# Moving twenty-eight places in the step table of a two-layer AdaLN kernel

## What is computed

```python
h = _layernorm(x) * (1 + ca) + sa
x = x + ga * _L0_attn_ref(h, ...)   # 16 heads of width 8, 4 key/value groups, relative-position bias, softmax
h = _layernorm(x) * (1 + cb) + sb
x = x + gb * _L0_ffn_ref(h, ...)    # routing: 4 of 16 experts; each silu(x W1 + b1) * (x W3 + b3), then W2
h = _layernorm(x) * (1 + ca) + sa   # layer 1
x = x + ga * _L1_attn_ref(h, ...)   # state-space layer: causal conv of 4, softplus step, scan over time, 256 x 16 states
h = _layernorm(x) * (1 + cb) + sb
x = x + gb * _L1_ffn_ref(h, ...)    # three matrices in a row (folded into one here), tanh
```

## Time and profile before

| | us |
|---|---|
| median of three runs | 2800.82 |
| profiled execution | 2800.82 |
| its span, first to last instruction | 2798.9 |
| PE busy | 2359.9 (84%) |
| DVE busy | 1940.0 (69%) |
| POOL busy | 1736.1 (62%) |
| ACT busy | 1631.4 (58%) |

### The profile page before, as it was taken

One profiled execution on the slowest core, in us unless ns is written; L12 is line 12 of the kernel. 1 busy time (PEld: TensorE's weight loads), 2 busy tenths in 40 slices (PEclk: granted clock), 3 DMA queues, 4 the chain that ended last, 5 costly groups with the idle time before them and its releaser, 6 DMA issues. The chain is left out here.

```text
span 2798.9 us, 37099 instructions
## 1 busy us (share of the span) xinstructions
PE 2359.9 (84%) x9792; PEld 1213.6 (43%) x9792; DVE 1940.0 (69%) x3181; ACT 1631.4 (58%) x4156; POOL 1736.1 (62%) x2247
## 2 busy tenths in 40 slices
PE   5889998989898999989889898989899998958433
PEld 3555544444444444444444444444444444422100
DVE  3444567686777768686776768686786868666776
ACT  3655566666666666666666666666666665533332
POOL 1012257585867858585866758586785857587543
PEclk9999999999999999999999999999999999978665
DMA  7424374665546565565546456555656465333442
GB/s 137 48 43 77 58 141 96 122 121 128 117 98 126 110 138 103 118 122 128 112 91 133 99 121 123 121 117 108 123 102 144 104 121 114 107 91 91 113 122 68
DMA packets 497981, 304.96 MB, mean 109 GB/s; under 512 B 349818, under 2 KB 416298, under 8 KB 497322
## 3 DMA queue, kind: packets, MB, share of 16 engines
q1 hardware_dynamic: 497772, 302.59, 52.9%
HBM read 242.21 MB, written 26.74 MB: 96 GB/s over the span
## 5 line engine op out<-in xcount | busy, mean ns | idle before, releaser
L1128 POOL TENSOR_TENSOR work<-work,bc 128x512 f32<-128x512 f32 x512 | 650.3, 1278 | 104.9 <-PE bank L1164 82.4
L1134 DVE TENSOR_TENSOR_SCAN work<-bank,work 128x512 f32<-128x512 f32 x512 | 621.2, 1213 | 109.3 <-POOL work L1128 83.5
L873 POOL TENSOR_TENSOR zh<-zh,w_bc 128x512 f32<-128x512 f32 x256 | 326.8, 1277 | 581.9 <-DVE zh L866 579.5
L1141 POOL TENSOR_TENSOR work<-work,bc 128x512 f32<-128x512 f32 x448 | 581.2, 1303 | 74.9 <-DVE work L1134 74.9
L1117 ACT ACTIVATE bank<-work,neg_a 128x510 f32<-128x510 f32 x512 | 351.5, 687 | 460.8 <-DVE work L1134 448.5
L532 PE MATMUL bank<-ke,q_all 96*128 96x256 f32 x2048 | 555.2, 395 | 12.0 <-DMA q_all<-q_rows 12.0
L549 ACT ACTIVATE probs<-bank,nmax 128x256 f32<-128x256 f32 x1024 | 473.6, 470 | 134.0 <-DVE nmax L539 131.9
L539 DVE TENSOR_REDUCE nmax<-bank 128x2 f32<-128x512 f32 x512 | 348.7, 681 | 233.0 <-PE bank L532 221.9
L532 PEld LDWEIGHTS bank<-ke,q_all 96*128 96x128 f32 x2048 | 382.1, 197 | 214.1 <-issue 163.2
L860 PE MATMUL bank<-h_b,w_t 128*128 128x512 f32 x512 | 297.4, 664 | 118.0 <-DVE zh L851 102.2
L559 PEld LDWEIGHTS bank<-ident,probs 128*128 128x128 f32 x2048 | 255.5, 144 | 242.6 <-issue 168.1
(11 more groups left out here) (192 smaller groups left out, 2528.4 us busy)
## 6 DMA issues: line engine op xcount, KB each, us to landing
work<-dt_rows SPq DMA_DIRECT2D x256, 512.0 KB, 5.3
w_bc<-w_rows_d SPq DMA_DIRECT2D x256, 256.0 KB, 4.4
ke<-ke SPq DMA_DIRECT2D x128, 256.0 KB, 5.0
bc<-bc_rows SPq DMA_DIRECT2D x64, 256.0 KB, 6.6
x_in<-in_x SPq DMA_DIRECT2D x32, 256.0 KB, 5.0
q_all<-q_rows SPq DMA_DIRECT2D x512, 8.0 KB
dt_rows<-step SPq DMA_DIRECT2D x16, 512.0 KB, 3.7
dt_rows<-step SPq DMA_DIRECT2D x32, 256.0 KB, 2.4
```

The lines of the kernel that those rows point to most:

```text
L873: nc.gpsimd.tensor_tensor(zh[:, n % 3, :], zh[:, n % 3, :], w_bc[:, n % WB, :], ALU.mult).then_inc(m_p, 1)
L1128: nc.gpsimd.tensor_tensor(hb[at % HB], ring[n % RING][:, 1, :], bc[:, s, :], ALU.mult).then_inc(s_dbx, 1)
L1134: nc.vector.tensor_tensor_scan(hb[at % HB], decay_bank(p, m)[:, :], hb[at % HB], 0.0, ALU.mult, ALU.add).then_inc(s_h, 1)
L1141: nc.gpsimd.tensor_tensor(hb[at % HB], hb[at % HB], bc[:, SG + batch(m)[2], :], ALU.mult).then_inc(s_hc, 1)
```

## The change

Only numbers of the table change (and the first and last step of the loop). 28 pieces get another step, most by one or two. In the order of the engines: on SP `x_a`, `x_res`, `a_store`, `m_fetch` and `f_store`; on PE `a_inverse`, `a_query`, `a_back`, `b_turned`, `m_weights`, `s_rows` and `f_turned`; on ACT `s_decay` (all 512 decays one step later), `a_keys`, `a_values_in`, `b_turned`, `m_weights`, `m_end` and `s_norm`; on DVE `s_end`, `m_up` (all 256 one step earlier), `a_end`, `s_silu` and `s_step`; on POOL `a_root`.

```diff
-            a_out_tensor=[79, 144], a_out_scalar=[79, 145], s_end_vector=[447, 499],
+            a_out_tensor=[79, 144], a_out_scalar=[79, 145], s_end_vector=[448, 500],
...
-            a_query_tensor=-34, f_end_tensor=531, a_back_tensor=148, b_turned_tensor=157, m_logits_tensor=164,
...
+            a_query_tensor=-33, f_end_tensor=531, a_back_tensor=150, b_turned_tensor=159, m_logits_tensor=164,
...
-            f_mix_tensor=527, s_decay_scalar=-1, m_tanh_scalar=2, a_turn_scalar=8, a_exp_scalar=3, a_values_scalar=42,
...
+            f_mix_tensor=527, s_decay_scalar=0, m_tanh_scalar=2, a_turn_scalar=8, a_exp_scalar=3, a_values_scalar=42,
...
-            a_max_vector=1, m_up_vector=4, m_silu_vector=2, a_inverse_vector=34, a_scale_vector=42, a_stats_vector=-88,
...
+            a_max_vector=1, m_up_vector=3, m_silu_vector=2, a_inverse_vector=34, a_scale_vector=42, a_stats_vector=-88,
```

More of the change, by code:

```diff
@@ L266, in build @@
         GROUP_STEPS = 4 * CPG
-        FIRST, LAST = -101, STEPS * (PAIRS - 1) + 535
+        FIRST, LAST = -102, STEPS * (PAIRS - 1) + 538
         AT = dict(
-            a_out_tensor=[79, 144], a_out_scalar=[79, 145], s_end_vector=[447, 499],
-            a_spread_sync=[[-28, -28, -12, 4], [20, 36, 52, 68]], a_scatter_sync=[[-22, 4], [37, 69]], x_a_sync=-99,
-            x_res_sync=107, a_store_sync=-34, m_store_sync=178, m_fetch_sync=-13, s_rows_sync=377,
-            s_rows_in_sync=[378, 380, 384, 386], s_store_sync=[372, 374], s_fetch_sync=-14, f_store_sync=531,
+            a_out_tensor=[79, 144], a_out_scalar=[79, 145], s_end_vector=[448, 500],
+            a_spread_sync=[[-28, -28, -12, 4], [20, 36, 52, 68]], a_scatter_sync=[[-22, 4], [37, 69]], x_a_sync=-100,
+            x_res_sync=104, a_store_sync=-35, m_store_sync=178, m_fetch_sync=-11, s_rows_sync=377,
+            s_rows_in_sync=[378, 380, 384, 386], s_store_sync=[372, 374], s_fetch_sync=-14, f_store_sync=534,
@@ L280, in build @@
[L280 to L283 removed]
+            a_inverse_tensor=42, s_sum_tensor=6, a_turned_tensor=-48, a_keys_tensor=-42, a_values_in_tensor=-37,
@@ new lines, in build @@
+            a_query_tensor=-33, f_end_tensor=531, a_back_tensor=150, b_turned_tensor=159, m_logits_tensor=164,
+            m_weights_tensor=178, m_back_tensor=326, s_turned_tensor=340, s_in_x_tensor=[348, 356], s_step_tensor=[364, 365],
+            s_rows_tensor=374, s_in_z_tensor=[390, 397], f_out_tensor=508, f_back_tensor=513, f_turned_tensor=524,
+            f_mix_tensor=527, s_decay_scalar=0, m_tanh_scalar=2, a_turn_scalar=8, a_exp_scalar=3, a_values_scalar=42,
+            a_norm_scalar=-51, a_turned_scalar=-42, a_keys_scalar=-40, a_values_in_scalar=-35, a_query_scalar=-33,
@@ L291, in build @@
-            f_root_gpsimd=517, s_step_vector=[366, 370],
+            s_silu_vector=[352, 360], s_zgate_vector=[392, 401], f_res_vector=514, f_stats_vector=518, f_end_vector=533,
+            s_read_gpsimd=4, m_weigh_gpsimd=5, s_input_gpsimd=-3, a_root_gpsimd=-83, b_root_gpsimd=155, s_root_gpsimd=330,
+            f_root_gpsimd=517, s_step_vector=[364, 368],
         )
```

9 lines of the change are left out of this document (3 added, 6 removed).

## The result

The changed kernel takes 2827.82 us (median of seven runs, 2815.03 to 2832.09), the kernel before 2800.41 us in the seven runs beside them (2788.27 to 2810.37). The ratio is 1.0102, with a 95% interval of 1.0074 to 1.013. The change made the kernel slower by 1%. The forecast of 2795 us is wrong, and wrong in its direction.

What follows compares the result with a forecast made beforehand. PE was taken as nearly full (146.90 of 160 us), with the chain to `b_turned` and DVE's routing barring shorter pairs. Sum: 2800.8 + 3 (regular pairs) + 5 (clock) - 14 (lock) = 2795 us; range 2764 to 2828.

Steps and rivals of the forecast that it cites:

- the clock's: Behind PE's wait ahead of `b_turned`: clock may halve, losing 1.7 us, in one pair in four: +5 us, bounds 0 and +20.
- The rival of 2828: Clock falls ahead of the routing in every second pair, and the up ahead of MAX meets slow PE: +27, chance 0.14.
- The wait itself: PE's wait ahead of `b_turned`: gains of 0.46 (`a_back`) and 0.7 us (earlier up) lengthen it from 1.12 to about 1.9.
- `h_b` ahead of the tanh, +0.6: On ACT: the copy delays the tanh, the silu and the routing stretch, +0.6 us a pair, bounds 0.3 and 0.8.
- the up ahead of MAX, +0.3: On DVE: the up, moved ahead of three small pieces, may meet PE still at work: 0 to +0.7 us, taken as +0.3.
- the tanh ahead of its decay, -0.6: End of the routing: the silu no longer waits 0.61 us for the tanh, -0.6 us a pair, bounds -0.6 and 0.
- The up ahead of the scan, +0.4: On DVE: it now waits for PE's up, where it waited 0.77 us for POOL: +0.4 us a pair.
- The slack that should have taken up two thirds of the loss: DVE's 2.0 us of idle time in the next stretch absorbs two thirds of +0.7 us, leaving +0.2 a pair.
- The lock, -14: DVE and POOL's shared lock: L1173 leaves the offset that stalls it, saving 3 x 4.8, about -14 us; bounds -14 and +55.
- `f_turned`, 0, and the step sizes, 0: PE's 0.48 us ahead of `f_turned` turns up again behind a decay; step sizes' later DVE work is covered by idle time.
- Over 160: a new wait repeats in each pair: Sign that the forecast is wrong: pairs over 160 us apart, where 157.3 plus or minus 1 was expected.
- The rival of closing waits: Four waits of PE close: -52 us, 2749, if all go, about 2766 with half and the stalls gone; chance 0.28.

Runs made afterwards that it cites:

- e1_fill: The changed kernel with twelve identity transposes on TensorE ahead of `b_turned`, where it would wait: 2788.28 us, 0.994 to the kernel before.
- e8_nodecay: The changed kernel with `s_decay_scalar` back at its old number, -1, and nothing else: 2819.27 us, 1.0061 to the kernel before.
- e3_back148: The changed kernel with `a_back_tensor` back at its old place, 148: 2822.08 us, 1.0072 to the kernel before.
- e7_back150: The kernel before with `a_back` alone moved behind the transposes (`a_end` and `b_turned` renumbered, which moves nothing): 2809.56 us, 1.0012.
- e5_decay0: The kernel before with the decay's number alone changed, so ACT puts an expert's tanh ahead of the decays: 2843.51 us, 1.0147.
- e6_hb: The kernel before with `h_b` copied ahead of the tanh of the 13th expert (`b_turned_scalar` 159): 2805.43 us, 1.0033.
- e2_up4: The changed kernel with DVE's up back at its old number (`m_up_vector` 4): 2828.74 us, 1.0064 to the kernel before.
- e4_up3: The kernel before with the number of DVE's up alone changed (`m_up_vector` 3): 2795.1 us, 0.998.
- e12_fill2: The changed kernel with twelve identity transposes ahead of `b_turned` and eight ahead of the routing weights: 2787.46 us, 0.9959 to the kernel before.
- e10_fill4: The changed kernel with four identity transposes ahead of `b_turned`: 2799.11 us, 0.9995 to the kernel before.
- e13_nodecayw: The changed kernel with `s_decay_scalar` back at -1 and eight identity transposes ahead of the routing weights: 2799.03 us, 0.9994 to the kernel before.
- e9_bfill: The kernel before with twelve identity transposes on TensorE ahead of `b_turned`: 2796.99 us, 0.9987.

## Why the prediction was wrong

**The step that failed is the clock's.** "One pair in four: 12/4 x 1.7 = +5 us." The mechanism, the place and the wait of 1.9 us were named; the sum then took a quarter of the pairs. Eleven of twelve fell. Measured by e1_fill: the twelve pairs take 1901.3 us with the filler and 1931.4 without, so the clock costs +30 us in them, 2.5 a pair. The other mistake in the term is its price. 1.7 us is the work lost in one slow stretch, and that is what one of 3.4 us costs (1.6); but seven of the eleven are twice as long (6.8 us) and cost 3.2. In eight of the eleven the 14th expert's up is slow besides, all or in part, which costs up to 0.9 more. The argument against the rival, that PE may be slowed in the scores alone, is refuted by the gate's 2.08 us.

The trace of before held what was needed. All pairs are copies of each other, so a wait that comes once comes in every pair. The fall does not come in every one: in the kernel before, the wait of about 2.23 us ahead of the 14th expert's up stands in all twelve pairs and the clock falls behind it in eight. That rate was there to be counted, and a quarter had no basis. The trace also had a price for a fall that is not hidden: its pair of 160.3 us (875.2 to 1035.5) has no stall. There the clock held behind the 2.23 us and fell at the up behind the weights, as in e8_nodecay. PE and the window, kernel before:

```profile
902.47 1.12 PE L860 MATMUL bank<-h_b,w_t 128*128 128x512 f32 x2 [2.23 <-DVE zh L851]
...
913.01 2.07 PE L860 MATMUL bank<-h_b,w_t 128*128 128x512 f32 x2 [1.29 <-DVE zh L851]
```
```profile
912.30:919.00 6.70, 5.99 (x14) 3.94 (x14) 4.46 (x5) 4.17 (x13) 6.70 (x7) 0.50 0.54 141
```

That is 3.0 us for one fall (0.66 of it may be L1173, at 1.81 us in this pair), not 1.7 in one pair of four. The rival of 2828 (0.14) had the right cause and nearly the measured time, partly by luck. Its falls in every second pair were too few. Its 0.7 for an up ahead of MAX that meets a slow PE is real (0.9, e1_fill), but does not come in every pair, and it does not say what its second 0.7 stands for.

**The wait itself** was forecast at about 1.9 and came at 1.97. Its working was half wrong: `a_back`'s 0.46 us has no part in it (e3_back148: 1.94, e7_back150: 1.10). The move of the tanh makes all of it (e5_decay0: 1.93, e8_nodecay: 1.09), by bringing the tanh 1.6 us and the up 0.8 us forward against a chain that starts when it starts. The gain of `a_back` stands ahead of the 12th expert's up instead.

**`h_b` ahead of the tanh, +0.6; the up ahead of MAX, +0.3; the tanh ahead of its decay, -0.6.** Together they were +0.3. e6_hb shows 0 for the first alone: its 0.6 took a later tanh for a later routing, and the pair did not lengthen. The other two show in the start of the up behind the weights, in pairs in which the 14th expert's up is fast. Before, it starts 37.81 us behind the pair's end. In e2_up4, which has the tanh ahead of its decay but not the up ahead of MAX, it starts at 37.07, so that term is -0.7. In e1_fill, which has both, it starts at 37.61, so the up ahead of MAX costs 0.5. Where the 14th expert's up is slow, the two starts are 37.47 and 38.55, and it costs 1.1. The prediction had 0 and 0.7 for these two cases: the difference between them was right, the level was 0.5 too low.

**The up ahead of the scan, +0.4.** Right: the next up starts 44.8 us behind the pair's end in e1_fill, 44.4 before. It (L862 in e1_fill) waits 1.10 us where L860 waited 0.61. The one after it waits 1.53 where it was 0.95. From e1_fill's timeline, against the second group, which is the timeline of the kernel before:

```profile
1547.23 1.13 PE L862 MATMUL bank<-h_b,w_t 128*128 128x512 f32 x2 [1.10 <-DVE zh L853]
1555.86 0.70 PE L862 MATMUL bank<-h_b,w_t 128*128 128x512 f32 x1 [1.53 <-DVE zh L853]
```
```profile
1877.97 1.12 PE L860 MATMUL bank<-h_b,w_t 128*128 128x512 f32 x2 [0.61 <-DVE zh L851]
1886.03 1.12 PE L860 MATMUL bank<-h_b,w_t 128*128 128x512 f32 x2 [0.95 <-DVE zh L851]
```

The slack that should have taken up two thirds of the loss did not: a pair is 0.8 to 0.9 us longer, and the prediction had 0.2. In twelve pairs e1_fill lies 13.7 us above 12 x 157.3 (1901.3 - 1887.6), where the prediction had +3. Some 5.5 of them are falls further back, one at the up behind the weights (1.7) and five at the 14th expert's (0.3 to 1.0); the rest, some 8, is the order, and by e2_up4 it is the up's number.

**The lock, -14.** Right in size: the two stalls in the twelve pairs had cost 11.4 us, the third lay in the filling, and L1173 has no 4.8 left (e4_up3, e2_up4: the up's number does it). The sum took 4.8 us for a stall where the text beside it read 5.5 from the pairs. In a stall L1173 takes 3.7 us longer (4.82 against 1.15), and the pair 5.5 to 6.0. The rest goes with the clock, which falls behind each stall. Window of the kernel before, behind the stall at 1399.07:

```profile
1403.60:1410.50 6.90, 4.25 (x10) 2.75 (x11) 6.64 (x9) 3.01 (x9) 3.81 (x4) 0.51 0.00 1
```

What the sum lacked is that leaving the bad offset is not the same as leaving POOL. L1173 starts at the very moment at which POOL begins an operation, and takes 1.81 us. DVE, then POOL, in the changed kernel:

```profile
1576.04 1.81 DVE L1173 SCALAR_TENSOR_TENSOR z_gate<-x_slots,d_par,z_gate 128x512 f32<-128x512 f32 x1
```
```profile
1574.80 1.27 POOL L1128 TENSOR_TENSOR work<-work,bc 128x512 f32<-128x512 f32 x1
1576.04 2.94 POOL L1141 TENSOR_TENSOR work<-work,bc 128x512 f32<-128x512 f32 x2
```

1.81 is one operation of POOL (1.26) and 0.55 us behind its end; before, L1173 took 1.15 in most pairs. That is 0.66 us a pair and would make nearly all of the 8 us, but no run parts it from the wait for the scan.

**`f_turned`, 0, and the step sizes, 0.** Both right as far as the traces go: `f_turned` waits for nothing now and the decay behind it still 0.57 us for its scan; L995 waits 2.86 us and the silu behind it 1.17, with no gap in the pair that answers to it.

**The sum again, from the runs.** -15.5 (two stalls 11.4, the fall in the pair of 160.3 3.0, rest) + 13.7 (the up's number some 8, falls further back 5.5) + 30.1 (the clock behind `b_turned`) = +28.3 us in twelve pairs, the measured difference. The range ended at 2828, the median was 2827.8. "Over 160: a new wait repeats in each pair" is the sign that came. The rival of closing waits fell as argued: all four waits shrank (0.94 to 0.36 us, 1.26 to 0.85, 0.48 to nothing, 1.29 to 0.58), and the time stood up again elsewhere, ahead of `b_turned` above all.

## What to carry to other kernels

In a kernel whose pieces repeat, a changed wait comes back in every round. What it sets off comes back in most: here the clock fell behind nearly the same wait (1.92 to 1.98 us) in 7, 8, 10 and 11 of twelve pairs in four kernels. Start from all rounds, and take a rate under one only from rounds counted in the trace. A gain on an engine that then waits for a chain of fixed length is not worth 0 where that engine is TensorE: its idle time may gather in one place, and what stands behind it may run at half the clock, as the gate did (2.08 us for 1.13). Where such a wait can't be closed, filling it with transposes into a free bank is worth a try, and then look at the next place with waits, since a fall that is prevented here may come back there (e8_nodecay).

## What the runs showed of the hardware

- The falls of the clock ahead of the gate, by the wait ahead of `b_turned`: 0.54 us, none in 24 pairs (e1_fill, e12_fill2); 1.08 to 1.14, none in 72 (the kernel before and five runs); 1.41, 3 in 12 (e10_fill4); 1.92 to 1.98, 36 in 48 (the changed kernel 11, e5_decay0 10, e3_back148 8, e2_up4 7). But behind 1.69 us ahead of the 12th expert's up there was none in 36 (e7_back150, e8_nodecay, e13_nodecayw). Which of two equal waits is hit was not settled.
- The clock also fell behind waits of 1.11, 0.71 and 0.82 us with short work between them, in every pair of e8_nodecay. The Trainium skill, TensorE: Matmul & The Clock Gate, "A second HAM failure mode: psum-queue depth-cycling", tells of another kernel in which PE idles briefly between groups of matmuls, often enough that the clock swings between its two levels. The rows of e8_nodecay agree.
- A fall may be harmless, and the order of another engine decides that. Behind the 2.23 us of the 14th expert's up the clock is 0.50 both before and after, in most pairs. Before, pairs with a slow up there and nothing else take 157.3 to 157.4 us, and the one pair without any fall 157.2. With DVE's up ahead of MAX the same fall costs 0.9 us (e1_fill, 158.1 and 159.0).
- L1173 (751 ns alone) took 1.14, 1.27, 1.81 or 4.8 us, by where it started against POOL's operations; in each case it ended 0.55 us behind the end of one of them. In the kernel before, the 4.8 came only at a start some 0.6 us ahead of the end of POOL's operation. Why it then lets three more pass, and eight other times in the kernel before does not, stays open.
- The filler of twelve transposes costs 1.47 us of TensorE and nothing in time: e9_bfill, whose wait of 1.12 us is shorter than the filler, starts `b_turned` within 0.04 us of where it was and its pairs stay at 157.3.
